# Three edits in the expert stage of a two-layer language-model tower: order of two VectorE steps, a GpSimd instruction, the last tile's second product

## The reference, cut to what matters

```
    top_w, top_i = jax.lax.top_k(probs, K)                 # K = 2 of E = 8
    ...
    padded = jnp.zeros((E, cap, D), x.dtype).at[se, pos].set(xf[pt])
    hidden = gelu(einsum('ecd,edh->ech', padded, w1) + b1)     # 192 -> 768
    out = einsum('ech,ehd->ecd', hidden, w2) + b2              # 768 -> 192
    expert_out = out[se, pos] * pw[:, None]
    final = jnp.zeros((T, D), x.dtype).at[pt].add(expert_out)
    h = h + final
```

## Time and profile before

| what | us |
|---|---|
| median of 3 runs | 849.3 (848.83 to 850.4) |
| the profiled execution, its own time | 850.6 |
| its span in the trace | 848.8 |
| first `up` after the last step of the dense layers that stands between tiles | 692.43 |
| last `up` (tile 38) begins | 824.71 |
| last addition is issued | 838.64 |
| mean granted TensorE clock | 0.972 |

### The profile page before, as it was taken

How to read it: one execution, slowest core, us unless ns; L and a number is a source line. 1 busy time by engine, 2 the same in 40 slices (tenths; PEclk the granted TensorE clock), 3 DMA queues, 4 the chain that set the end, 5 groups by cost and what they waited for, 6 DMA issues and landing times.

```text
span 848.8 us, 16016 instructions
## 1 busy us (share of the span) xinstructions
PE 745.0 (88%) x5742; PEld 553.9 (65%) x5743; DVE 507.8 (60%) x1714; ACT 302.3 (36%) x698; POOL 231.3 (27%) x281
## 2 busy tenths in 40 slices
PE   1898777989889998978999898899989999999992
PEld 0546455566557656655755675667857998898892
DVE  7558668773779787367976546882355633333330
ACT  0033142533444262434326244334334433333330
POOL 5332110442002346101321200132001554433342
PEclk9999989999999999999999999999999999999997
DMA  7960000000000100000010000018501332222220
GB/s 245 415 279 1 1 1 1 19 8 1 2 2 6 52 20 8 1 2 1 25 33 1 1 2 2 1 39 302 165 2 29 58 71 44 38 43 35 37 32 8
DMA packets 29447, 43.11 MB, mean 51 GB/s; under 512 B 5099, under 2 KB 24277, under 8 KB 29382
## 3 DMA queue, kind: packets, MB, share of 16 engines
q1 hardware_dynamic: 19122, 30.87, 10.5%
q0 software_dynamic: 8432, 8.53, 5.8%
q10 hardware_dynamic: 1828, 2.84, 1.0%
HBM read 20.81 MB, written 22.09 MB: 51 GB/s over the span
## 4 chain that ended last, share of the span: by engine, by line
PE 55%; DVE 25%; issue 6%; DMA 4%; ACT 4%; POOL 4%; SPq 1%; DVEq 0%; POOLq 0%; ACTq 0%
PE qa L1915 25%; PE qc L1915 23%; PE qc L1918 4%; PE qa L1918 3%; DMA out<-qk_T 3%; DVE mx L1493 2%; DVE st L1064 2%; DMA mu_row<-in_mu 1%; ACT big L818 1%; POOL arena_w L438 1%; DVE xb L1108 1%; DVE qk_T L1499 1%; POOL rs_a L473 1%; DVE arena_e L1305 1%; DVE ctxT L1448 1%
## 5 line engine op out<-in xcount | busy, mean ns | idle before, releaser
L1915 PE MATMUL qc<-arena_w,big 128*128 x468 | 82.9, 327 | 1.7 <-DVE qk_T L1894 1.4
L1915 PEld LDWEIGHTS qc<-arena_w,big 128*128 128x128 f32 x468 | 75.1, 190 | 2.6 <-issue 2.5
L1915 PE MATMUL qa<-arena_b 128*128 128x128 f32 (+2 forms) x688 | 71.4, 283 | 1.0 <-ACT arena_b L775 0.8
L1915 PE MATMUL qa<-arena_e,nT 128*128 128x192 f32 (+2 forms) x256 | 68.7, 423 | 2.3 <-DVE ga L1375 2.0
L1030 ACT ACTIVATE big<-qa,arena_b 128x128 f32<-128x128 f32 x156 | 43.1, 375 | 73.9 <-PE qc L1915 69.0
L1915 PEld LDWEIGHTS qa<-arena_b 128*128 128x128 f32 (+2 forms) x688 | 62.9, 186 | 9.6 <-issue 2.3
L615 POOL DMA_INDIRECT out<-qk_T x39 | 63.0, 1617 | 20.1 <-POOL spare L614 11.5
L1883 DVE COPY arena_b<-qc 128x256 f32<-128x256 f32 x39 | 16.6, 426 | 78.4 <-PE qc L1918 78.4
L1915 PEld LDWEIGHTS qa<-arena_e,nT 128*128 128x128 f32 x256 | 45.9, 195 | 24.2 <-issue 14.1
L473 POOL TENSOR_TENSOR rs_a<-rs_a,minus_half 128x8 f32<-128x8 f32 x4 | 6.6, 1644 | 171.3 <-DVE rs_a L1342 171.3
L1918 PE MATMUL qa<-cst,arena_b 128*128 128x128 f32 (+2 forms) x232 | 34.6, 291 | 9.3 <-DVE arena_e L1305 3.7
(11 more groups left out here) (393 smaller groups left out, 1587.1 us busy)
## 6 DMA issues: line engine op xcount, KB each, us to landing
slots<-xk SPq DMA_DIRECT2D x1, 13192.0 KB, 42.6
arena_e<-in_w SPq DMA_DIRECT2D x8, 579.0 KB, 7.8
arena_w<-in_w SPq DMA_DIRECT2D x8, 576.0 KB, 9.5
qk_T<-slots SPq DMA_DIRECT2D x39, 97.0 KB, 1.9
out<-hb SPq DMA_DIRECT2D x16, 96.0 KB, 1.7
arena_e<-in_w_l SPq DMA_DIRECT2D x1, 804.0 KB
arena_e<-in_W ACTq DMA_DIRECT2D x1, 768.0 KB
out<-qk_T POOLq DMA_INDIRECT x39, 3.6
```

The source lines that it names most:

```text
L1915: return nc.tensor.matmul(o, l, r, start=start, stop=stop)
```

## The change

It does three things.

1. In `evacuate` the two DVE steps for tile T+2 change places: `stage_w1` stands ahead of `xT_evac`.
2. `add` on POOL loses its carrying instruction, with the semaphore `carried` and the wait on it; the indirect DMA follows the waits for `m_y` and `m_add`. POOL's tiles 12 to 38 are no longer a hardware loop with register arithmetic for the waits and a ring position, but are written out.
3. For tile 38 alone, `gelu` raises `m_gelu` after each of its six activations and not once at the end, and `down` waits for it ahead of each of its six products.

```diff
             def add(tile, u, turn):
                 pool.wait_ge(m_y, tile + 1)
-                since(pool, carried, tile)
                 since(pool, m_add, tile * 16)
-                pool.tensor_tensor(spare[:, 0:1], minus_half[:, 0:1], minus_half[:, 0:1], ALU.add).then_inc(carried, 1)
                 pool.indirect_dma_start(
...
-            tiles(pool, add)
+            for tile in range(EARLY, MT):
+                add(tile, tile % RING, tile // RING)
             pool.wait_ge(m_add, 16 * MT)
...
             def gelu(tile, u, turn):
                 act.wait_ge(m_up, tile + 1)
                 since(act, m_down, tile - 1)
+                last = isinstance(tile, int) and tile == MT - 1
                 for j in range(FJ):
                     i = A(hTm[:, u % 2, j, :], PS[u % 2][:, j % 2, j // 2 * 128:j // 2 * 128 + 128], ACT.Gelu,
                           bias=w1s[u % 3][:, F + FJ // 2 * 128 + j:F + FJ // 2 * 128 + j + 1])
-                i.then_inc(m_gelu, 1)
+                    if last or j == FJ - 1:
+                        i.then_inc(m_gelu, 1)
...
             def evacuate(tile, u, turn):
                 if more(tile, 2):
+                    stage_w1(tile + 2, (u + 2) % RING)
                     xT_evac(tile + 2, (u + 2) % RING)
-                    stage_w1(tile + 2, (u + 2) % RING)
                 if more(tile, -1):
                     weight(tile - 1, (u - 1) % RING)
...
             def down(tile, u):
                 expert = pe.value_load(own_i[0:1, bass.ds(tile, 1)], min_val=0, max_val=NE - 1)
+                last = isinstance(tile, int) and tile == MT - 1
                 pe.wait_ge(m_gelu, tile + 1)
                 since(pe, m_y, tile)
                 for j in range(FJ):
+                    if last and j:
+                        pe.wait_ge(m_gelu, tile + 1 + j)
                     i = mm(PD[:, 1, 0:D], hTm[:, u % 2, j, :],
```

More of the change, by code:

```diff
@@ L87, in build @@
             sem(n) for n in ("fills", "setup_v", "setup_p", "setup_a", "slots_empty"))
-        route, scattered, carried = (
-            sem(n) for n in ("route", "scattered", "carried"))
+        route, scattered = (
+            sem(n) for n in ("route", "scattered"))
         slot_in = [sem(f"slot_in{u}") for u in range(RING)]
```

## The result

The changed kernel takes 845.66 us (median of 13 runs, 843.11 to 847.91) beside 848.91 of the kernel before (13 runs, same chip): ratio 0.9946, 95% interval 0.9928 to 0.9964. A second time it was 848.11 (12 runs) beside 849.9 (30 runs), ratio 0.9982, 0.9962 to 1.0002. The profiled execution took 846.09 by its own time. The forecast was 842.5, its range 840.7 to 847.1: the first median lies in it, the second does not, and its interval reaches 1.

What follows compares the result with a forecast made beforehand. PE was taken to be bound by its weights' wait for DVE's copy, at the very end by the chain of additions; 5.4 + 1.4 = 6.8 us off the median 849.3 gave 842.5, range 840.7 to 847.1.

Steps and rivals of the forecast that it cites:

- the forecast's own range: Whole kernel: gains of 7.8 down to 5.5 us, thus 841.5 to 843.8, before the medians' spread and a rival were added.
- the first rival: Additions on POOL: release to issue stays 0.88 us, 4.6 each, never catching up with PE; 847.1 us, chance 0.10.
- Part 1: Tile loop: with the copy ahead of the evacuation, PE's period falls from 4.62 to 4.53 us; gain 5.4 us.
- Cover of the copy: DVE in the loop: copy and evacuation end before PE's next `up` needs them, about 1.4 us of cover left.
- Part 2: Last additions on POOL: without the carrying instruction they are issued sooner; gain 1.4 us, between 0.6 and 1.8.
- x: POOL: distance from an addition's release to its issue, now 0.88 us; taken as 0.45, bounds 0.29 and 0.70 or 0.88.
- Rival two: Tile loop: PE's own order sets 4.62 us, the earlier copy gains nothing, POOL's 1.4 remains; 847.9 us, chance 0.05.
- Rival three: POOL: the copy holds each addition for its whole length; 858.9 us, or about no change; chance 0.06.
- the priced 0.2: POOL in the loop: us added to each addition's issuing where it meets the copy, taken as hidden.
- Part 3: Last tile's `down` on PE: chunks free nothing, five added waits cost 0 to 0.26 us, hidden; gain nought.
- the end: Behind the last landing: 7.0 us of drain on POOL, left as it is.

Runs made afterwards that it cites:

- pe_code_moved_70: The changed kernel with 70 already met waits added at PE's start, moving PE's later code; ratio 0.9978 to the kernel before.
- pool_only: The kernel before with only POOL's change: no carrying instruction, POOL's tiles written out; ratio 0.9988 to the kernel before.
- swap_only: The kernel before with only the weights' copy put ahead of the evacuation on DVE; ratio 0.9926 to the kernel before.
- swap_unrolled_carrier: The kernel before with the copy ahead of the evacuation and POOL's tiles written out, the carrying instruction kept; ratio 0.9922 to the kernel before.
- waits_moved_160: The changed kernel with an addition's two waits in the other order and 160 already met waits at PE's start; timed on its second run, ratio 0.9918.

## Why the prediction was right or wrong

The direction and the source of most of the gain were right; the size was not, 6.8 against 2.8 by the stage. That 845.66 falls in the range (840.7 to 847.1) is in part luck: the forecast's own range ended at 843.8, the rest was added for the first rival, which went another way than the kernel did, and the second median, 848.11, is outside. The three misses add up: 0.6 + 1.2 + 2.3 = 4.1.

- **Part 1, 5.4.** Right in its mechanism and nearly in size: 126.77 where nothing disturbs, 127.41 and 127.56 in the two profiles of the kernel after, so 4.9 and 4.7. The single pair of rows at tiles 10 and 11 did give PE's own period. What was not seen: the first tiles behind 10 can be held by late additions through the ring of six (shown in pe_code_moved_70; in the kernel after it is the likely cause of its 0.57).
- **Cover of the copy.** Forecast to end at 1.24 behind `weight`, 1.7 at the loop's start: 1.27 in steady state (809.81 to 811.08). At a turn the copy waited up to 1.19 us for ACT, and the evacuation was still not late.
- **Part 2, the step that failed.** x was taken as 0.45, "nearer to the row of the same form", because an indirect DMA at the kernel's start stood 0.29 behind a wait. It measured 0.77 to 0.83. That row was a gather, its sequencer awake; the row that told was the idle 0.52 behind `spare`, which "the trace ascribes to nothing". It goes with the indirect DMA, since it is 0.72 where the carrying instruction is gone (after, pool_only); what it consists of no run shows. With x = 0.83 the tail without the late landing would be: 35 issued at 819.65 (both its release times are 818.8), 36 at 824.07, 37 at 828.33, 38 at 831.87, 13.73 behind the last `up`, 1.2 more than the forecast's 12.54.
- **The first rival, x stays**, was thus right in its cause and wrong in its consequence, though its 2.2 us of gain are nearer to the measured 2.8 than the forecast's 6.8. It let the additions fall behind with 4.6 us each. They took (815.22 - 730.53)/19 = 4.46, since they landed after 3.6 and not 3.7, and kept up with 4.53. That its number came near is luck: the late landing of 34, which it did not have, took back what it had missed. The chance of 0.10 was too low for its cause.
- **The tail's landing of 34** had no term: 16.02 against those 13.73 makes 2.3. It is an effect of part 1: PE leaves its loop earlier against the additions, and a fetch that came 0.6 behind their packets before now meets them (swap_only has it, pool_only has not).
- **Rival two**, PE gains nothing, is out by swap_only. **Rival three**, the copy holds the addition: the additions beside a copy took 1.55 to 1.91, one before tile 10 took 2.03, against 1.55, so the priced 0.2 was fair, up to 0.36 on `weight`'s release. Nothing came near 0.77.
- **Part 3** nought, **the end** of the program unchanged: both right (10.1 behind the last issue).

On the rule of the Trainium skill (SBUF — State Buffer, "Who interferes with whom": whoever comes second is fully blocked), which the prediction said the trace does not agree with: where the copy came second it kept its 0.77, and it was the addition, the first, that grew. Where the addition came second the trace is nearer to the rule. Timeline of the kernel after, the copy and, in POOL's, the addition that began inside it:

```profile
796.73 0.77 DVE L1890 COPY arena_b<-arena_e 128x1158 f32 x1 [0.51 <-issue]
```

```profile
797.00 1.91 POOL L613 DMA_INDIRECT out<-qk_T  x1 [2.62 <-DVE qk_T L1895]
```

They share 0.50 us (797.00 to 797.50) and the addition is 0.36 longer than 1.55. The same holds for every addition from tile 16 on that began inside a copy: it grew by the overlap less 0.11 to 0.14 (overlap 0.26, 0.38, 0.45, growth 0.12, 0.24, 0.32 at 751.97, 810.70, 792.51). So with the copy first the rule nearly holds; with the addition first it does not: two additions that began 0.12 and 0.13 ahead of a copy (761.01, 788.17) kept their 1.55, and the copies their 0.77.

What stays open: what the 0.72 consists of; where PE's fetch comes (it moved by 1.4 us against the last `up` in swap_unrolled_carrier, in which PE's code is that of swap_only); why a fetch at the end of the packets costs a whole microsecond more, and once nothing; and why the ratios on the slower chips (0.9926 for swap_only, 6.5 us) are lower than the stage says (some 3 us). Between the profiled executions of pool_only and swap_only the times (873.18 and 869.85) do differ as the stages do (146.56 and 143.09); the medians are 4.6 apart. That the fetch meets the addition in some executions only would explain it, but each kernel has one or two profiles, so it is not shown.

## What to carry to other kernels

When a faster engine has won its time, follow the next chain landing by landing to the program's end, and price it from release to issue in the same state, not from another place where the instruction stood behind work. An idle stretch with no releaser in front of a DMA is a cost that stays until an experiment moves it. Where one stage repeats and the part before it drifts, measure from a landmark in the stage: it told 2.8 us where two ratios said 4.6 and 1.5.

## What the runs showed of the hardware that was not expected

- An indirect DMA that adds 128 rows of 768 bytes needs 0.72 us between the sequencer's MOVE and its start on POOL (after, pool_only, waits_moved_160), 1.55 for issuing, and lands 3.4 to 3.9 after it starts (2.7 in the last two). One that must wait for the landing before it has a period of about 4.2 to 4.6 us (tiles 11 to 17 of the kernel after: 4.16 to 4.45).
- A fetch of 16 KB of PE's code can delay the landing of another queue's DMA by 2 us (gaps of 6.39 to 6.79 against 4.47), and adding waits on PE that are already met moves it: the tail falls from 16.02 to 14.2. The Trainium skill (Runtime: NRT & Kernel Launch, "Instruction fetch mechanics") gives blocks of 16 KiB, and holds the fetch to be mostly hidden; the size agrees with the one packet of 0.02 MB in the profile, and PE itself did not stall (its next product began 820.44, 2.30 behind the last `up`, the same distance as in the loop), but a DMA beside it did.
- In the hardware loop (PE's part runs from 704.95 to 813.8) such fetches of q8 show only in its first 21 us: none lies between 726 and 819 in the trace of the kernel after; the next comes some 5 us after PE's last product of the loop (it ends at 811.67 + 2.12 = 813.79).
